# One cross attention of an eight-layer chain: four score products issued together, new instruction orders, and its last normalisation moved to GpSimd

## The chip, the core and the metric

One Trainium2 chip, one core. The metric is the device time of one execution in microseconds (us). The kernel does a whole chain of layers in one launch; the change touches a single phase of it, the cross attention called L1.

The engines have these names in the profile: PE is TensorE (matrix products), PEld its weight loads, DVE is VectorE, ACT is ScalarE, POOL is GpSimd. Each engine works through its own instruction list in order, and waits on semaphores that the others raise.

## The reference

x is 32 tiles of 128 tokens by 128 features, and ctx is of the same shape. The chain adds to x, layer by layer, a cross attention and a feed-forward network, four times. The L1 cross attention is:

```
q = layernorm(x) @ Wq.T ;  k = ctx @ Wk.T ;  v = ctx @ Wv.T      (16 heads of 8)
p = softmax(q k.T / sqrt(8))                                      (128 x 128 for each head)
x = x + concat(p v) @ Wo.T
```

The network that follows starts from layernorm(x), and this phase makes that normalised x too.

## The kernel before

All 32 tiles of x lie in on-chip memory (X). The phase `cross_attention_L1` works on one batch entry (a "tile", 128 x 128) at a time, and it is software-pipelined by hand. On every engine a function `step(n, ...)` lists the operations of one turn, each with its own offset: `maxima(n - 1, ...)` is the maxima of tile n-1, `norm(n + 1, ...)` the normalisation of tile n+1. `sequence_loop(engine, 32, lead, lag, step)` runs the turns. So the order of an engine is what `step` lists, and the offset says which tile it is for. Each helper waits on the semaphores of what it needs, and on those that say that the buffer it writes is free (most buffers have two copies, w = tile mod 2).

One tile goes through these operations (function, engine, line before):

- `statistics`, `aggregate` (DVE, L752, L757): mean and variance of a tile of x. `log_variance`, `over_deviation` (ACT, L696, L701): one over the deviation, through a logarithm and an exponential. `norm` (DVE, L763): the normalised tile; it waits for `over_deviation` of the same tile.
- `turn_x` (PE, L868): transpose. `evacuate_x` (DVE, L770): copy out of PSUM. `project` (PE, L875 to L877): q, k, v. `evacuate_fixed`, `evacuate_spread`, `evacuate_values` (DVE, L776, L782, L788): copies of the three. `turn_x` of the next tile waits for `evacuate_values` of this one, since both use one PSUM bank. `spread_heads`, `block_values`, `fetch_context` (POOL, L677, L670, L663): layouts for the products.
- `scores` (PE, L886): four products, one for each group g of four heads, into PSUM banks 0 to 3. Product g reads 32 rows of the array (rows 32g to 32g+31). The banks exist once, so product g of tile b needs the exponentials of group g of tile b-1 to be done.
- `maxima` (DVE, L794): row maxima of a group. `exponentials` (ACT, L719): four instructions for a group.
- `turn_probs` (PE, L897): four transposes for a group, into PSUM bank 4 or 5. `evacuate_probs`: copy out, for groups 0, 1, 2 on ACT (L728), for group 3 on DVE (L801).
- `weighted_values` (PE, L911): 64 small products; it needs all four copies. `one_over_rows`, `evacuate_heads` (DVE, L808, L814), `output` (PE, L919), `residual` (DVE, L819): x is updated.
- `statistics2`, `aggregate2` (DVE, L824, L829), `log_variance2`, `over_deviation2` (ACT, L706, L711), `end_norm` (DVE, L834): the normalised x for the next network.

Of the kernel before, what the change touches and what calls it, by code (L numbers as in the profile page):

```python
# [21 lines left out]
ALU = mybir.AluOpType  # L22
# [4 lines left out]
P = 128  # L27
# [548 lines left out]
def cross_attention_L1(nc, env, a):  # L576
# [55 lines left out]
    xn2_ready = sem("xn2_ready")  # L632
    probT3_ready = sem("probT3_ready")
# [15 lines left out]
    with nc.Block() as block:  # L649
# [5 lines left out]
        def _(pool):  # L655
# [23 lines left out]

            def step(n, u, live):  # L680
                v = 1 - u
                block_values(n, u, live)
                fetch_context(n + 1, v, live)
                spread_heads(n + 1, v, live)
            sequence_loop(pool, NB, 1, 0, step)
# [3 lines left out]
        def _(act):  # L689
# [18 lines left out]
            def over_deviation2(b, w, live):  # L708
                if live(b):
                    act.wait_ge(lnvar2_ready, b + 1)  # L710
                    nc.scalar.activation(rstd2[:, w:w + 1], lnvar2[:, w:w + 1], ACT.Exp, scale=-0.5).then_inc(rstd2_ready, 1)  # L711
# [19 lines left out]
            def step(n, u, live):  # L731
                v = 1 - u
                evacuate_probs(n + 1, v, 1, live)
                exponentials(n + 1, v, 3, live)
                log_variance(n + 4, u, live)
                over_deviation(n + 4, u, live)
                log_variance2(n - 1, v, live)
                evacuate_probs(n + 1, v, 2, live)
                over_deviation2(n - 1, v, live)
                exponentials(n + 2, u, 0, live)  # L740
                exponentials(n + 2, u, 1, live)
                exponentials(n + 2, u, 2, live)
                evacuate_probs(n + 2, u, 0, live)
            sequence_loop(act, NB, 4, 1, step)

        @block.vector
        def _(dve):
# [78 lines left out]
            def aggregate2(b, w, live):  # L826
                if live(b):
                    wait_alone(dve, env, stats2_ready, b + 1)
                    nc.vector.bn_aggr(moments2[:, w, :], stats2[:, w, :]).then_inc(moments2_ready, 1)  # L829

            def end_norm(b, w, live):
                if live(b):
                    dve.wait_ge(rstd2_ready, b + 1)
                    nc.vector.tensor_scalar(tile_of(NORMED, b), tile_of(X, b), moments2[:, w, 0:1], rstd2[:, w:w + 1],  # L834
                                            ALU.subtract, ALU.mult).then_inc(xn2_ready, 1)

            def step(n, u, live):
                v = 1 - u
                residual(n - 3, v, live)
                evacuate_values(n - 1, v, live)  # L840
                statistics2(n - 3, v, live)
                aggregate2(n - 3, v, live)
                statistics(n + 2, u, live)
# [4 lines left out]
                aggregate(n + 2, u, live)  # L848
                evacuate_x(n, u, live)
                maxima(n - 1, v, 3, live)  # L850
                one_over_rows(n - 2, u, live)
                evacuate_spread(n, u, live)
                evacuate_heads(n - 2, u, live)
                evacuate_fixed(n, u, live)
                end_norm(n - 4, u, live)
                norm(n + 1, v, live)
            sequence_loop(dve, NB, 2, 4, step)

        @block.tensor
        def _(pe):  # L860
# [18 lines left out]
            def scores(b, w, half, live):  # L879
                if live(b):  # L880
                    pe.wait_ge(spread_ready, b + 1)
                    pe.wait_ge(fixed_ready, b + 1)
                    for g in (2 * half, 2 * half + 1):
                        wait(pe, exp_ready, 4 * (b - 1) + g + 1)
# [36 lines left out]
            def step(n, u, live):  # L921
                v = 1 - u
                output(n - 3, v, live)
                turn_probs(n - 2, u, 2, live)
                scores(n - 1, v, 0, live)
                turn_x(n, u, live)
                turn_probs(n - 2, u, 3, live)
                scores(n - 1, v, 1, live)
                weighted_values(n - 2, u, live)
                project(n, u, live)  # L930
                turn_probs(n - 1, v, 0, live)
                turn_probs(n - 1, v, 1, live)
            sequence_loop(pe, NB, 0, 3, step)
# [2312 lines left out]
```

## Time and profile before

| | |
|---|---|
| median of three runs | 4469.63 us (4464.69 to 4471.03) |
| the profiled execution | 4465.72 us, span 4463.9 us |
| mean granted TensorE clock of the span | 0.96 |
| the L1 phase in the span | 307.6 to 560.3 us |
| PE, DVE, ACT, POOL busy in the span | 4153.5, 3762.2, 3604.0, 3147.1 us |

A timeline row is: start, busy time, engine, line, operation, output <- inputs, shapes, and how many like it were merged; in brackets the idle time before it and what ended it. Instructions overlap on one engine at their ends, so the time that one takes from the engine is read from start to start, while its length says when its result is there. The granted clock (PEclk) is 1.00 at 2.4 GHz and 0.50 at 1.2 GHz.

### The profile page before, as it was taken

The page shows a single profiled execution, that of the slowest core. Times are in us where ns is not written, and L with a number is a line of the kernel's source. Part 1 is how long each engine was busy: PE and PEld are TensorE (multiplying, and loading weights), DVE is VectorE, ACT ScalarE, POOL GpSimd, SP SyncE. Part 2 cuts the span into 40 slices and gives each one's busy share as a digit, 9 for nine tenths or more (in the row PEclk, how much of TensorE's full clock was granted, in tenths as well). Part 3 has the DMA queues.
Part 4 walks back from the last instruction along what each step waited for, and adds up shares of the span by engine and source line. Part 5 has one row for each costly group of instructions (what it writes and reads, how often), then busy time and mean ns, then how long its engine had stood idle before and what let it go on. Part 6 is the DMA issues. An engine that isn't in the chain of part 4 may idle for free. (4 is left out here: it accounts for less than half of the span.)

```text
span 4463.9 us, 151456 instructions
## 1 busy us (share of the span) xinstructions
PE 4153.5 (93%) x51003; PEld 2751.8 (62%) x51005; DVE 3762.2 (84%) x9029; ACT 3604.0 (81%) x12939; POOL 3147.1 (71%) x4201
## 2 busy tenths in 40 slices
PE   6949999999999999999999999999999999677885
PEld 3426656666666666666666666666666666455543
DVE  4779989889889889889888889889889885788497
ACT  6938878888888888888888888888888887688335
POOL 2422288888888888889888888888888885444162
PEclk9969999999999999999999999999999999788886
DMA  2000000000000000000000000000000000000000
GB/s 64 0 21 1 0 8 2 2 3 17 13 2 2 2 21 8 2 3 7 17 8 2 2 12 12 8 2 3 17 12 2 2 2 2 1 0 0 30 0 20
DMA packets 38631, 37.27 MB, mean 8 GB/s; under 512 B 11382, under 2 KB 30068, under 8 KB 37748
## 3 DMA queue, kind: packets, MB, share of 16 engines
q1 hardware_dynamic: 38004, 28.97, 2.3%
q8 instruction: 386, 6.32, 0.6%
q14 instruction: 241, 1.97, 0.1%
HBM read 26.86 MB, written 2.10 MB: 6 GB/s over the span
## 5 line engine op out<-in xcount | busy, mean ns | idle before, releaser
L2326 ACT ACTIVATE stack_prob<-ps,stack_shift_by 128x128 f32<-128x128 f32 x3072 | 1081.2, 378 | 3.3 <-DVE stack_shift_by L2448 2.7
L2254 POOL TENSOR_TENSOR stack_qk<-stack_qk,stack_rsin 128x512 f32<-128x512 f32 x768 | 970.8, 1275 | 41.1 <-DVE stack_rsin L2473 41.0
L2261 POOL TENSOR_TENSOR stack_qk<-stack_qk,stack_inv 128x512 f32<-128x512 f32 x768 | 794.8, 1046 | 217.8 <-ACT stack_inv L2345 217.8
L2646 PE MATMUL ps<-local_wqkv,stack_xsT 128*128 128x512 f32 x1536 | 797.1, 601 | 4.5 <-DVE stack_rsin L2473 2.4
L2268 POOL TENSOR_TENSOR stack_prob<-stack_prob,stack_rs 128x512 f32<-128x512 f32 x768 | 793.0, 1044 | 1.7 <-DVE stack_rs L2455 1.7
L2326 ACT ACTIVATION_READ_ACCUMULATOR stack_prob<-ps,stack_shift_by 128x1 f32 x3072 | 671.3, 219 | 1.3 <-issue 1.3
L2448 DVE TENSOR_REDUCE stack_shift_by<-ps 128x4 f32<-128x512 f32 x768 | 524.0, 682 | 77.2 <-PE ps L2725 71.9
L2473 DVE TENSOR_TENSOR stack_rsin<-ps,stack_sin_t 128x256 f32<-128x256 f32 x1536 | 571.9, 413 | 4.7 <-issue 4.7
L2462 DVE TENSOR_TENSOR stack_qk<-ps,stack_cos_t 128x512 f32<-128x512 f32 x768 | 525.2, 684 | 37.1 <-ACT stack_sq L2334 36.1
L2480 DVE TENSOR_REDUCE stack_ss<-stack_sq 128x8 f32<-128x512 f32 x768 | 513.3, 669 | 0.7 <-ACT stack_sq L2334 0.7
L2334 ACT ACTIVATE stack_sq<-ps 128x512 f32<-128x512 f32 x768 | 468.4, 610 | 52.8 <-PE ps L2646 45.3
L2306 ACT ACTIVATE stack_probT<-ps 128x512 f32<-128x512 f32 x768 | 428.7, 632 | 12.0 <-PE ps L2756 11.6
L2663 PE MATMUL ps<-local_wqkv,stack_xvT 128*128 128x512 f32 x768 | 432.9, 646 | 3.0 <-issue 3.0
L2776 PEld LDWEIGHTS ps<-stack_probT,stack_vals 128*64 128x64 f32 x6144 | 328.2, 136 | 162.2 <-issue 149.5
L2776 PE MATMUL ps<-stack_probT,stack_vals 128*64 128x128 f32 x6144 | 420.8, 279 | 5.8 <-issue 4.0
L2300 ACT ACTIVATE stack_qkT<-ps 128x512 f32<-128x512 f32 x384 | 231.4, 603 | 236.9 <-PE ps L2693 236.9
L2791 PE MATMUL ps<-local_wo,stack_oT 128*128 128x128 f32 x3072 | 389.0, 280 | 0.2 <-issue 0.2
L2791 PEld LDWEIGHTS ps<-local_wo,stack_oT 128*128 128x128 f32 x3072 | 361.2, 192 | 34.3 <-issue 24.5
L2646 PEld LDWEIGHTS ps<-local_wqkv,stack_xsT 128*128 128x128 f32 x1536 | 258.7, 191 | 173.4 <-issue 94.5
L2725 PE MATMUL ps<-stack_qkT 64*64 64x64 f32 (+1 forms) x12288 | 339.4, 230 | 0.0
L2725 PEld LDWEIGHTS ps<-stack_qkT 64*64 64x64 f32 x12288 | 307.2, 134 | 0.0
L2756 PEld LDWEIGHTS ps<-ident,stack_prob 64*128 64x128 f32 x6144 | 222.4, 139 | 93.9 <-issue 90.2
(342 smaller groups left out, 8606.0 us busy)
## 6 DMA issues: line engine op xcount, KB each, us to landing
local_wqkv<-L_ffn_Wqkv SPq DMA_DIRECT2D x30, 256.0 KB, 2.7
local_wo<-L_ffn_Wo SPq DMA_DIRECT2D x6, 512.0 KB, 4.6
out<-quantised_res SPq DMA_DIRECT2D x8, 256.0 KB, 2.3
local_w<-L_ffn_W SPq DMA_DIRECT2D x6, 341.0 KB
local_wqkv<-L_ffn_Wqkv SPq DMA_DIRECT2D x1, 1536.0 KB, 6.3
early_L_decay<-c_decay SPq DMA_DIRECT2D x1, 1024.0 KB, 10.0
local_w<-L_ffn_W SPq DMA_DIRECT2D x12, 64.0 KB
load_raw<-L_ffn_w SPq DMA_DIRECT2D x8, 64.0 KB, 1.9
```

What stands on the lines that cost most here:

```text
L2254: nc.gpsimd.tensor_tensor(qk[w][:, j, :, :], qk[w][:, j, :, :], rsin[j % 2][:, :, :], ALU.add).then_inc(rot_ready, 1)
L2261: nc.gpsimd.tensor_tensor(qk[w][:, j, :, :], qk[w][:, j, :, :], bcast(inv[:, w, 8 * j:8 * j + 8].unsqueeze(2), [P, 8, LH]), ALU.mult).then ...
L2268: nc.gpsimd.tensor_tensor(prob[w][:, g, :, :], prob[w][:, g, :, :], bcast(rs[:, w, HG * g:HG * g + HG].unsqueeze(2), [P, HG, P]), ALU.mult ...
L2326: last = nc.scalar.activation(prob[w][:, g, j, :], ps[:, 4 + g % 2, j * P:(j + 1) * P], ACT.Exp, bias=shift_by[:, w, h:h + 1], accum_out=s ...
L2448: nc.vector.tensor_reduce(shift_by[:, w, HG * g:HG * g + HG], bank, AX, ALU.max, negate=True).then_inc(shift_by_ready, 1)
L2462: nc.vector.tensor_tensor(qk[w][:, j, :, :], bank, bcast(cos_t[:, j // 2, :].unsqueeze(1), [P, 8, LH]), ALU.mult)
L2473: last = nc.vector.tensor_tensor(rsin[j % 2][:, :, o], bank[:, :, x], bcast(sin_t[:, j // 2, o].unsqueeze(1), [P, 8, 32]), ALU.mult)
L2480: nc.vector.tensor_reduce(ss[:, w, 8 * j:8 * j + 8, 0], sq[j % 2][:, :, :], AX, ALU.add).then_inc(ss_summed, 1)
L2646: nc.tensor.matmul(proj_bank(j), xsT[w][:, :], wqkv[:, 512 * j:512 * j + 512], start=True, stop=True).then_inc(proj_ready, 1)
L2725: last = nc.tensor.matmul(ps[part, 4 + p, j * P + keys.start:j * P + keys.stop], qkT[w][r, half, 0, j, part], qkT[w][r, half, 1, j, keys], ...
L2776: last = nc.tensor.matmul(PV[LH * p:LH * p + LH, j * P:(j + 1) * P], vals[w][:, LH * h:LH * h + LH], probT[w][:, 2 * half + p, j, :], star ...
L2791: last = nc.tensor.matmul(OUT[:, 0:P], oT[w][:, c, :], wo[:, c, :], start=c == 0, stop=c == 7)
```

## The change

1. `scores(b, w, half)` was called twice in a turn, for two groups each, with other PE work in between. Now `scores(b, w)` is called once, issues the four products one after the other, and first waits for all four exponentials of the tile before.
2. `end_norm` leaves DVE. POOL does it in two operations, a subtraction into a new buffer `centred` and a multiplication. Its semaphore is now also waited for by `aggregate2` and `over_deviation2`.
3. The lists of `step` on all engines are written anew, with new offsets.

```
@@ pool @@
+            def end_norm(b, w, live):
+                if live(b):
+                    pool.wait_ge(moments2_ready, b + 1)
+                    nc.gpsimd.tensor_tensor(centred[:, w, :], tile_of(X, b), bcast(moments2[:, w, 0:1], [P, P]),
+                                            ALU.subtract).then_inc(centred_ready, 1)
+                    wait_alone(pool, env, rstd2_ready, b + 1)
+                    wait_alone(pool, env, centred_ready, b + 1)
+                    nc.gpsimd.tensor_tensor(tile_of(NORMED, b), centred[:, w, :], bcast(rstd2[:, w:w + 1], [P, P]),
+                                            ALU.mult).then_inc(xn2_ready, 1)
             def step(n, u, live):
                 v = 1 - u
+                spread_heads(n + 1, v, live)
+                fetch_context(n + 2, u, live)
                 block_values(n, u, live)
-                fetch_context(n + 1, v, live)
-                spread_heads(n + 1, v, live)
-            sequence_loop(pool, NB, 1, 0, step)
+                end_norm(n - 3, v, live)
+            sequence_loop(pool, NB, 2, 3, step)
@@ scalar, over_deviation2 @@
+                    wait(act, xn2_ready, b - 1)
@@ scalar, step @@
-                evacuate_probs(n + 1, v, 1, live)
-                exponentials(n + 1, v, 3, live)
-                log_variance(n + 4, u, live)
-                over_deviation(n + 4, u, live)
-                log_variance2(n - 1, v, live)
-                evacuate_probs(n + 1, v, 2, live)
-                over_deviation2(n - 1, v, live)
                 exponentials(n + 2, u, 0, live)
                 exponentials(n + 2, u, 1, live)
                 exponentials(n + 2, u, 2, live)
                 evacuate_probs(n + 2, u, 0, live)
-            sequence_loop(act, NB, 4, 1, step)
+                exponentials(n + 2, u, 3, live)
+                evacuate_probs(n + 2, u, 1, live)
+                log_variance(n + 5, v, live)
+                evacuate_probs(n + 2, u, 2, live)
+                over_deviation(n + 5, v, live)
+                log_variance2(n, u, live)
+                over_deviation2(n, u, live)
+            sequence_loop(act, NB, 5, 0, step)
@@ vector, step (end_norm taken out above) @@
-                residual(n - 3, v, live)
-                evacuate_values(n - 1, v, live)
-                statistics2(n - 3, v, live)
-                aggregate2(n - 3, v, live)
-                statistics(n + 2, u, live)
                 maxima(n - 1, v, 0, live)
                 evacuate_probs(n - 2, u, 3, live)
                 maxima(n - 1, v, 1, live)
                 maxima(n - 1, v, 2, live)
-                aggregate(n + 2, u, live)
-                evacuate_x(n, u, live)
+                evacuate_spread(n, u, live)
                 maxima(n - 1, v, 3, live)
+                evacuate_fixed(n, u, live)
+                evacuate_values(n, u, live)
                 one_over_rows(n - 2, u, live)
-                evacuate_spread(n, u, live)
                 evacuate_heads(n - 2, u, live)
-                evacuate_fixed(n, u, live)
-                end_norm(n - 4, u, live)
-                norm(n + 1, v, live)
-            sequence_loop(dve, NB, 2, 4, step)
+                statistics(n + 3, v, live)
+                aggregate(n + 3, v, live)
+                norm(n + 2, u, live)
+                residual(n - 2, u, live)
+                evacuate_x(n + 1, v, live)
+                statistics2(n - 2, u, live)
+                aggregate2(n - 2, u, live)
+            sequence_loop(dve, NB, 3, 2, step)
@@ tensor @@
-            def scores(b, w, half, live):
+            def scores(b, w, live):
...
-                    for g in (2 * half, 2 * half + 1):
-                        wait(pe, exp_ready, 4 * (b - 1) + g + 1)
+                    wait_alone(pe, env, exp_ready, 4 * b)
+                    for g in range(G):
...
             def step(n, u, live):
                 v = 1 - u
-                output(n - 3, v, live)
-                turn_probs(n - 2, u, 2, live)
-                scores(n - 1, v, 0, live)
-                turn_x(n, u, live)
+                scores(n - 1, v, live)
                 turn_probs(n - 2, u, 3, live)
-                scores(n - 1, v, 1, live)
+                project(n, u, live)
                 weighted_values(n - 2, u, live)
-                project(n, u, live)
+                turn_x(n + 1, v, live)
                 turn_probs(n - 1, v, 0, live)
                 turn_probs(n - 1, v, 1, live)
-            sequence_loop(pe, NB, 0, 3, step)
+                output(n - 2, u, live)
+                turn_probs(n - 1, v, 2, live)
+            sequence_loop(pe, NB, 1, 2, step)
```

What this does to the order is seen best at the start of the phase, where the tiles can be counted. First DVE, from the last `norm` (L763, writes xn) ahead of the first maxima (L794, write shift_by) to the next `norm`, before the change. The first row is the norm of tile 1, the maxima are those of tile 0, and the last row is the norm of tile 2:

```order
L763 TENSOR_SCALAR L_cross_xn<-X,L_cross_moments,L_cross_rstd 128x128
L788 COPY L_cross_vals<-ps 128x128
L752 BN_STATS L_cross_stats<-X 128x6
L794 TENSOR_REDUCE L_cross_shift_by<-ps 128x4 x3
L757 BN_AGGR L_cross_moments<-L_cross_stats 128x2
L770 COPY L_cross_xnT<-ps 128x128
L794 TENSOR_REDUCE L_cross_shift_by<-ps 128x4
L782 TENSOR_SCALAR L_cross_spread_src<-ps 128x128
L776 COPY L_cross_fixed<-ps 128x128
L763 TENSOR_SCALAR L_cross_xn<-X,L_cross_moments,L_cross_rstd 128x128
```

The same piece of DVE after the change (norm is now L777, maxima L808). Three norms stand ahead of the first maxima, so the first row is the norm of tile 2, and the last row, which follows the maxima of tile 0, is the norm of tile 3:

```order
L777 TENSOR_SCALAR L_cross_xn<-X,L_cross_moments,L_cross_rstd 128x128
L784 COPY L_cross_xnT<-ps 128x128
L808 TENSOR_REDUCE L_cross_shift_by<-ps 128x4 x3
L796 TENSOR_SCALAR L_cross_spread_src<-ps 128x128
L808 TENSOR_REDUCE L_cross_shift_by<-ps 128x4
L790 COPY L_cross_fixed<-ps 128x128
L802 COPY L_cross_vals<-ps 128x128
L766 BN_STATS L_cross_stats<-X 128x6
L771 BN_AGGR L_cross_moments<-L_cross_stats 128x2
L777 TENSOR_SCALAR L_cross_xn<-X,L_cross_moments,L_cross_rstd 128x128
```

So in one turn DVE now has maxima(b) and norm(b+3), where it had maxima(b) and norm(b+2). The copy of the values moved from the end of the list to just behind the copy of q.

Second ACT, before the change, from the `log_variance` and `over_deviation` of tile 2 (L696, L701) over the exponentials of tile 0 (L719) and the copies of the turned probabilities (L728) to the pair of tile 3:

```order
L696 ACTIVATE L_cross_lnvar<-L_cross_moments,eps 128x1
L701 ACTIVATE L_cross_rstd<-L_cross_lnvar 128x1
L719 ACTIVATE L_cross_prob<-ps,L_cross_shift_by 128x128 x12
L728 ACTIVATE L_cross_probT<-ps 128x512 x2
L719 ACTIVATE L_cross_prob<-ps,L_cross_shift_by 128x128 x4
L696 ACTIVATE L_cross_lnvar<-L_cross_moments,eps 128x1
L701 ACTIVATE L_cross_rstd<-L_cross_lnvar 128x1
L728 ACTIVATE L_cross_probT<-ps 128x512
```

The same piece of ACT after the change (L709 and L714 are the pair, L733 the exponentials, L742 the copies):

```order
L709 ACTIVATE L_cross_lnvar<-L_cross_moments,eps 128x1
L714 ACTIVATE L_cross_rstd<-L_cross_lnvar 128x1
L733 ACTIVATE L_cross_prob<-ps,L_cross_shift_by 128x128 x12
L742 ACTIVATE L_cross_probT<-ps 128x512
L733 ACTIVATE L_cross_prob<-ps,L_cross_shift_by 128x128 x4
L742 ACTIVATE L_cross_probT<-ps 128x512
L709 ACTIVATE L_cross_lnvar<-L_cross_moments,eps 128x1
L742 ACTIVATE L_cross_probT<-ps 128x512
L714 ACTIVATE L_cross_rstd<-L_cross_lnvar 128x1
```

The pair of tile 3 still stands behind the exponentials of tile 0; its second half, on which `norm` of tile 3 waits, moved behind the third copy as well, and the second copy moved behind the last exponentials.

## Rows read from the trace of the kernel before

**Rows 1.** Windows: length, busy us (instructions) of PE, PEld, DVE, ACT, POOL; clock

```profile
400.00:440.00 40.00, 39.91 (x556) 27.75 (x556) 38.14 (x98) 35.98 (x128) 9.66 (x30) 1.00 0.00 0
```

**Rows 2.** Timeline of PE, one tile in the middle of the L1 phase

```profile
427.63 1.19 PE L886 MATMUL ps<-L_cross_spread,L_cross_fixed 32*128 32x512 f32 x4
428.75 0.33 PE L868 MATMUL ps<-ident,L_cross_xn 128*128 128x128 f32 x1
428.91 0.60 PE L897 MATMUL ps<-ident,L_cross_prob 128*128 128x128 f32 x4
...
430.50 1.08 PE L911 MATMUL ps<-L_cross_probT,L_cross_vbd 128*32 128x128 f32 x32
...
432.39 0.49 PE L875 MATMUL ps<-L_cross_xnT,L1WqT 128*128 128x128 f32 x2
...
434.03 0.39 PE L919 MATMUL ps<-L1WoT,L_cross_oT 128*128 128x128 f32 x2
434.45 0.66 PE L897 MATMUL ps<-ident,L_cross_prob 128*128 128x128 f32 x4
435.03 1.13 PE L886 MATMUL ps<-L_cross_spread,L_cross_fixed 32*128 32x512 f32 x4
```

**Rows 3.** Timeline of DVE at the same place

```profile
426.56 0.98 DVE L834 TENSOR_SCALAR Y<-X,L_cross_moments,L_cross_rstd  x1
427.46 0.33 DVE L763 TENSOR_SCALAR L_cross_xn<-X,L_cross_moments,L_cross_rstd 128x128 f32 x1
427.72 0.27 DVE L819 TENSOR_TENSOR X<-X,ps 128x128 f32 x1
427.92 0.28 DVE L788 COPY L_cross_vals<-ps 128x128 f32<-128x128 f32 x1
428.12 0.28 DVE L824 BATCH_NORM_STATS2 L_cross_stats<-X 128x6 f32 x1
...
428.64 0.29 DVE L752 BATCH_NORM_STATS2 L_cross_stats<-X 128x6 f32 x1
428.89 0.69 DVE L794 TENSOR_REDUCE L_cross_shift_by<-ps 128x4 f32<-128x512 f32 x1
...
430.16 1.28 DVE L794 TENSOR_REDUCE L_cross_shift_by<-ps 128x4 f32<-128x512 f32 x2
431.36 0.17 DVE L757 BATCH_NORM_AGGREGATE L_cross_moments<-L_cross_stats 128x2 f32<-128x6 f32 x1
```

**Rows 4.** Timeline of ACT at the same place

```profile
426.40 1.09 ACT L728 ACTIVATE L_cross_probT<-ps 128x512 f32<-128x512 f32 x2 [0.66 <-PE ps L897]
427.37 1.15 ACT L719 ACTIVATE L_cross_prob<-ps,L_cross_shift_by 128x128 f32<-128x128 f32 x4
428.37 0.33 ACT L696 ACTIVATE L_cross_lnvar<-L_cross_moments,eps 128x1 f32<-128x1 f32 x1
428.73 0.20 ACT L701 ACTIVATE L_cross_rstd<-L_cross_lnvar 128x1 f32<-128x1 f32 x1
428.84 0.28 ACT L706 ACTIVATE L_cross_lnvar<-L_cross_moments,eps 128x1 f32<-128x1 f32 x1
429.02 0.58 ACT L728 ACTIVATE L_cross_probT<-ps 128x512 f32<-128x512 f32 x1
```

**Rows 5.** Timeline of POOL and DVE: the last normalisation beside and without a POOL operation

```profile
426.42 1.04 POOL L677 TENSOR_TENSOR L_cross_spread<-L_cross_spread_src,head_rows 128x512 f32<-128x512 f32 x1 [4.41 <-DVE L_cross_spread_src L782]
...
551.54 0.34 DVE L834 TENSOR_SCALAR Y<-X,L_cross_moments,L_cross_rstd 128x128 f32<-128x128 f32 x1
```

**Rows 6.** Groups of instructions, other attentions: four-row-group products; a 128x128 POOL operation

```profile
L1643 PE MATMUL ps<-L_cross_spread,L_cross_fixed 32*128 32x512 f32 x256 | 39.3, 685 | 6.2 <-POOL L_cross_spread_aux L1347 4.5 <-issue 1.0
...
L366 POOL TENSOR_TENSOR L_cross_xb<-X,early_L_b_o 128x128 f32<-128x128 f32 x32 | 14.6, 455 | 0.0
```

**Rows 7.** Windows: the middle of the L2 attention

```profile
3900.00:4100.00 200.00, 155.77 (x2436) 114.97 (x2439) 172.92 (x410) 175.35 (x315) 94.45 (x251) 0.87 0.00 0
```

**Rows 8.** Timeline of PE at the start of the L1 phase, before the clock rose

```profile
314.31 2.08 PE L886 MATMUL ps<-L_cross_spread,L_cross_fixed 32*128 32x512 f32 x4 [1.50 <-POOL L_cross_spread L677]
```

More of the change, by code:

```diff
@@ L632, in cross_attention_L1 @@
     xn2_ready = sem("xn2_ready")
+    centred_ready = sem("centred_ready")
+    centred = sb("centred", [P, 2, P])
     probT3_ready = sem("probT3_ready")
@@ L827, in aggregate2 @@
                 if live(b):
-                    wait_alone(dve, env, stats2_ready, b + 1)
+                    waits_alone(dve, env, (stats2_ready, b + 1), (xn2_ready, b - 1))
                     nc.vector.bn_aggr(moments2[:, w, :], stats2[:, w, :]).then_inc(moments2_ready, 1)
[L831 to L835, printed above, removed]
             def step(n, u, live):
                 v = 1 - u
-                residual(n - 3, v, live)
-                evacuate_values(n - 1, v, live)
-                statistics2(n - 3, v, live)
-                aggregate2(n - 3, v, live)
-                statistics(n + 2, u, live)
                 maxima(n - 1, v, 0, live)
```

## The prediction

> **What bounds the kernel now.** I read the L1 phase in three steps: the windows of its middle, then the timelines of PE, DVE and ACT over one tile, then the idle times in them. The windows say that PE is busy 39.91 of 40 us, DVE 38.14 and ACT 35.98, at full clock [rows 1]. One tile takes from one first score product to the next, 427.63 to 435.03, so 7.40 us [rows 2]. PE works through nearly all of it. The only hole is at its end: `output` starts at 434.03 and the next transposes only at 434.45, though the tile before them left little to do. They wait for ACT's copy of group 0, and ACT had sat idle 0.66 us before that copy, waiting for PE's transposes [rows 4]. PE is the bound, with about 0.2 us of wait. DVE is close behind, and something there is dearer than it looks: the last normalisation at 426.56 keeps DVE for 0.90 us until the next starts at 427.46 [rows 3], while the same operation at the end of the phase lasts 0.34 us; in the first case POOL was in its `spread_heads` from 426.42 to 427.46 [rows 5]. So L834 stood still until POOL was through, and about 0.64 of its 0.90 us is that wait (0.90 less 0.26, what `norm` next to it takes [rows 3]).
>
> **What the change takes away.** (a) Score products. Two calls a tile take 1.12 us of PE each (427.63 to 428.75) [rows 2]. Four products on four row groups, issued together, are not in the L1 trace, but the L2 attention has them: 39.3 us for its 32 tiles, so 1.23 us for all four [rows 6], with its clock partly low. Bounds: no gain if they ran pair after pair (2.24), and 1.12 us if they take what a pair takes now. I take 1.1. (b) DVE loses the last normalisation, 0.90 us a tile, 0.26 if nothing had stood in its way. (c) POOL gains two operations of 128x128; 14.6 us for 32 such, 0.46 us each [rows 6]. POOL is busy 9.66 of 40 us [rows 1], so 1.8 a tile and then 2.7: no bound.
> The Trainium skill, "SBUF — State Buffer", section "SBUF: two separate sides", says that VectorE in a two-port mode and GpSimd take one port pair in turn, for a whole instruction. The trace agrees with 0.90 us beside POOL and 0.34 us without. Where DVE is the bound, that rule alone would make (b) worth 0.9 us a tile; it is part of rival A.
>
> **What the new orders put in.** This decides, and no busy time shows it: the offsets. Before, DVE's turn held the maxima of tile b and the `norm` of tile b+2; now it holds the maxima of b and the `norm` of b+3. `norm(b+3)` waits for `over_deviation(b+3)`. On ACT that stands, as before, behind the exponentials of tile b, and now also behind its third copy. Before, DVE asked for a value that ACT had made a tile earlier. Now it asks for one that ACT makes at the end of the same tile, after sixteen exponentials that themselves start from DVE's maxima. And behind the waiting `norm` on DVE stand `residual`, `evacuate_x`, the two of `statistics2`, and the maxima of tile b+1. So the turn becomes a ring, maxima(b) to maxima(b+1). Its length, start to start:
>
> - DVE, from the first maxima to the copy of the values: maxima and probability copy 1.27 (428.89 to 430.16), two maxima 1.20 (430.16 to 431.36), `evacuate_spread` 0.2, the fourth maxima 0.6, `evacuate_fixed` 0.2, and `evacuate_values` with its whole 0.28 [rows 3]: 3.75. The two 0.2 are the residual's start-to-start time, 427.72 to 427.92, since all are 128x128.
> - PE: `turn_x` must wait for that copy (one bank), then 0.16 (428.75 to 428.91), then the four transposes of group 0 of tile b, 0.60 until their result is there [rows 2]; with 0.05 for the hand-over, 0.81.
> - ACT: that group's copy 0.49 (two take 0.97, 426.40 to 427.37), the last exponentials 1.00 (427.37 to 428.37), a copy 0.49, the logarithm 0.18 (428.84 to 429.02), a copy 0.49, the exponential 0.20 [rows 4]; 2.85, and 0.04 of hand-over. Could ACT be later by its own work? From the maxima it is 0.69, three groups of exponentials 3.0: 3.7, before the 4.6 at which PE is done. So it waits for PE, some 0.8 us.
> - DVE again: `norm` 0.26 (427.46 to 427.72), `residual` 0.20, `evacuate_x` 0.2, `statistics2` with `aggregate2` 0.52 (428.12 to 428.64) [rows 3]; 1.18 and 0.04.
>
> Sum: 3.75 + 0.81 + 2.89 + 1.22 = 8.67. Each operation that I rounded up could be 0.03 less, so I take 8.6 us for a tile, against 7.4: **+1.2 us**. What the four products save on PE lies beside the ring. They start when the last exponentials of tile b are done and take 1.2 us with their result, while ACT needs 0.49 + 0.18 + 0.49 + 0.20 = 1.36 us more and DVE 1.2 after that. DVE reaches the next maxima 1.2 us after the products are ready. The 0.9 us off DVE falls into the new wait too: DVE is busy 38.14 of 40 us [rows 1], 7.1 us in 7.4, and 6.2 without the 0.9; of 8.6 us it then idles 2.4, some 2 of them at `norm`.
> `norm` waits like this for tiles 3 to 31, 29 times: 29 x 1.2 = **+35 us**.
>
> **Smaller terms.** The start: until its clock rises PE takes 2.08 us for a pair of score products [rows 8], and PE bounds there; one pair less for each of the first tiles, partly eaten by the ring: -3. The end: after the last statistics POOL does two dependent operations of 0.46 [rows 6] where DVE did one of 0.34 [rows 5]: +1. The clock: in the middle of L1 PE is busy 39.91 of 40 us at 1.00 [rows 1]; in the L2 attention it is busy 155.77 of 200 us and is granted 0.87 [rows 7], so it was at 1.2 GHz for a quarter of the time. With about 6.3 us of work (7.4 less 1.1) in 8.6 PE will be like that or a little busier. At half clock the ring gets another leg: maxima and copy 1.27, weighted values 1.89 (430.50 to 432.39) [rows 2] doubled to 3.8, then `turn_x` and transposes 1.4, in all 6.5 until ACT can copy, where the ring above has 4.6: +1.9 us for such a tile. Bounds: none, or a quarter of 29 tiles with all of it, 14 us. I take a tenth: +6.
> "TensorE: Matmul & The Clock Gate" of the Trainium skill, section "HAM oscillation — how this bites in real kernels", says that short stretches of products between waits are throttled anew each time. The windows of L2 agree. By that alone the clock term would be the upper bound.
>
> Sum: 35 - 3 + 1 + 6 = **+39 us**. Against the profiled execution's own 4465.72 us that is 4505; the median of the runs shown is 4469.63, 3.9 above it, so a median would be about 4508. Predicted: **4507 us**.
>
> **Rivals.**
> A, faster. The `norm` wait does not bind, because DVE asks later or ACT answers earlier than I read. Then PE has 7.40 - 1.1 - 0.2 = 6.1, DVE 7.4 - 0.9 = 6.5, ACT 7.4 - 0.66 = 6.7; and the banks make a ring of their own, since all four products wait for the last exponentials: 1.2 for the products, 0.69 for the first maxima, 4.0 of exponentials, one copy 0.49, and 0.4 of hand-overs, 6.8. So about 6.9 us a tile, 31 x -0.5 = -15 us: 4455. It decides if the wait at `norm` is under about 0.9 us a tile (2 less 1.2). For it: busy sums all fall. Against it: the order, in which no `over_deviation(b+3)` can come before the exponentials of tile b. Chance 0.08.
> B, no change: the wait binds, but ACT waits less for PE and the ring closes near 7.4. That needs 1.2 us out of 8.6, more than the whole 0.8 us wait in it. 0.04.
> C, the clock. L2's 0.87 or less in L1, with PE's share in the ring doubled for a quarter to half of the tiles: 14 to 28 us instead of 6, 4515 to 4530. 0.13.
> The forecast: 0.75.
>
> **Numbers.** A measurement of this kernel can tell about 0.2% (9 us) from no change. Faster 0.08, within 0.2% 0.04, slower 0.88. The ring's bounds: 8.45 to 8.7 us, so 31 to 38 us, and the clock 0 to 14: 4469.6 + 31 - 3 + 1 = 4498 to 4469.6 + 38 + 14 = 4522. Leaving two in ten outside, half of them on the side of A, I widen to 4488 and 4524.
>
> **What would show it.** In the timeline of the changed kernel's L1 phase: a tile takes 8.6 us; DVE idles about 2 us a tile before `norm` (now L777), released by ACT's `over_deviation` (L714), and that is the longest wait of the phase. ACT idles twice, once at the copy of group 0 (released by PE) and once before the first exponentials (released by the maxima). The four score products start within some 0.02 us of each other or in a row with a result after 1.2 us. PE idles 2 us a tile and its clock falls at times. POOL's two new operations last 0.46 us. Wrong would be: no idle time at L777, or a tile under 7.4 us; then A holds. Products that run pair after pair would be hidden behind the ring (0.3 us of it at most would show). If the tile takes 8.6 but the time is off, it is the clock term.

## The result and the profile after

The changed kernel takes 4519.78 us (median of five runs, 4514.52 to 4522.26) against 4469.63 (five runs, 4464.69 to 4471.03): ratio 1.011, 95% interval 1.0099 to 1.0121. It is slower, by 50 us, where 37 were predicted (4507; the prediction's own sum of terms was 39). The span of its profiled execution is 4518.0 us, 54.1 more than before's.

Where the 54.1 lie was read from the first and the last instruction of each phase. The L1 phase runs from 307.7 to 609.4, so 301.7 us where it took 252.7: +49.0. The layer stack behind it, whose code is the same, takes 5.3 more. Every other part differs by 0.9 at most, and all of them together by -0.2.

The windows of the changed kernel, as in [rows 1] and [rows 7]: a piece of the middle, the long stretch of equal tiles, and L2.

```profile
440.00:480.00 40.00, 30.14 (x410) 21.29 (x408) 26.65 (x74) 28.39 (x100) 10.52 (x32) 1.00 0.00 0
...
335.00:585.00 250.00, 188.60 (x2667) 136.57 (x2655) 173.01 (x463) 179.67 (x631) 72.55 (x222) 0.99 0.00 0
...
3900.00:4100.00 200.00, 157.93 (x2399) 116.48 (x2399) 171.07 (x408) 173.95 (x308) 91.01 (x247) 0.86 0.00 1
```

PE was busy 39.91 of 40 us [rows 1] and is now busy 30.14; DVE fell from 38.14 to 26.65. No engine is busy all the time any more. The tile grew by waiting, so the next view is the list of waits of 335 to 590 us (engine, line, who released it: us in total, times, longest):

```profile
DVE L_cross_xn L777 <- ACT L_cross_rstd L714: 64.0, 27, 2.8
ACT L_cross_prob L733 <- DVE L_cross_shift_by L808: 49.8, 28, 2.1
...
ACT L_cross_probT L742 <- PE ps L904: 17.5, 28, 1.6
...
PE ps L875 <- DVE L_cross_vals L802: 12.7, 27, 0.5
```

For each tile DVE waits at `norm` (L777) for ACT, 2.4 us; ACT waits at the copy (L742) for PE's transposes; PE waits at `turn_x` (L875) for DVE's copy of the values. These are the three hand-overs of a ring: a chain of waits that leads back to its own start, one tile later. ACT's wait for the maxima follows from the first, since the maxima stand behind `norm` on DVE. The timelines show it closed. DVE, one whole tile:

```profile
443.13 0.69 DVE L808 TENSOR_REDUCE L_cross_shift_by<-ps 128x4 f32<-128x512 f32 x1
...
446.52 0.28 DVE L802 COPY L_cross_vals<-ps 128x128 f32<-128x128 f32 x1
...
450.83 0.34 DVE L777 TENSOR_SCALAR L_cross_xn<-X,L_cross_moments,L_cross_rstd 128x128 f32 x1 [2.35 <-ACT L_cross_rstd L714]
...
452.48 0.69 DVE L808 TENSOR_REDUCE L_cross_shift_by<-ps 128x4 f32<-128x512 f32 x1 [0.43 <-issue]
```

PE and ACT between them:

```profile
446.95 0.30 PE L875 MATMUL ps<-ident,L_cross_xn 128*128 128x128 f32 x1 [0.48 <-DVE L_cross_vals L802]
447.16 1.09 PE L904 MATMUL ps<-ident,L_cross_prob 128*128 128x128 f32 x8
...
449.70 1.14 PE L893 MATMUL ps<-L_cross_spread,L_cross_fixed 32*128 32x512 f32 x8 [0.46 <-ACT L_cross_prob L733]
```

```profile
447.93 0.60 ACT L742 ACTIVATE L_cross_probT<-ps 128x512 f32<-128x512 f32 x1 [0.63 <-PE ps L904]
448.42 1.13 ACT L733 ACTIVATE L_cross_prob<-ps,L_cross_shift_by 128x128 f32<-128x128 f32 x4
...
450.56 0.24 ACT L714 ACTIVATE L_cross_rstd<-L_cross_lnvar 128x1 f32<-128x1 f32 x1
```

DVE from the first maxima to the end of the copy: 443.13 to 446.80, 3.67. PE until ACT can copy group 0: to 447.93, 1.13. ACT until `norm` starts: to 450.83, 2.90. DVE until it could take the next maxima: to 452.05, 1.22. That is 8.92. Then it idles 0.43 more, released by nothing but "issue", and this row comes at every second tile only. One turn of the hardware loop covers two tiles (`sequence_loop` runs `step` for u = 0 and 1), which is why the loop is suspected; e7 tries it. The tile shown is 9.35 us from first maxima to first maxima, its neighbours without the idle time are 9.00, mean 9.18, where tiles had a mean of 7.37. (Read from `norm` to `norm` the same tiles are 8.94 and 9.41; the expectation of e7 has them so.) 27 waits x 1.81 = 49 us, as much as the phase grew.

### The profile page after: what moved, and what is told of

Its sections match the earlier page's. It is cut to its first block and busy times, and to the rows that moved or that the text cites. A ratio compares the mean times of both kernels' runs of the same rounds, so it can differ in the third digit from the quotient of the medians.

```text
span 4518.0 us, 151512 instructions
## 1 busy us (share of the span) xinstructions
PE 4141.5 (92%) x51003; PEld 2752.0 (61%) x51005; DVE 3738.5 (83%) x8997; ACT 3600.3 (80%) x12939; POOL 3165.2 (70%) x4265
## 5 line engine op out<-in xcount | busy, mean ns | idle before, releaser
L2699 PE MATMUL ps<-ident,stack_qk 64*128 64x64 f32 x6144 | 274.6, 229 | 7.9 <-issue 6.3
```

## The experiments

All times are medians. Ratios are against the kernel before, run beside them: it took 4469.75 us beside e1 to e4, 4474.41 beside e5 to e8 and 4468.58 beside e9 to e11, so runs of different groups are compared by their ratios. "A tile" is the mean, first maxima to first maxima, of twenty tiles in the middle (tiles 5 to 24) of the profiled execution, in the changed kernel without the one that met 1.2 GHz; before 7.37. "L1" is the length of that phase in the profile, before 252.7.

| run | what it is | us | ratio (95%) | L1 | a tile |
|---|---|---|---|---|---|
| changed kernel | | 4519.78 | 1.011 (1.0099 to 1.0121) | 301.7 | 9.18 |
| e1_dev_early | over_deviation a tile earlier | 4479.25 | 1.0021 (1.0011 to 1.003) | 260.7 | 7.76 |
| e2_turnx_late | turn_x behind two groups of transposes | 4498.43 | 1.0062 (1.0047 to 1.0078) | 279.0 | 8.48 |
| e3_both | e1 and e2 | 4462.25 | 0.9984 (0.9975 to 0.9993) | 243.4 | 7.10 |
| e4_both_pairs | e3, products in two pairs | 4492.19 | 1.0045 (1.0029 to 1.006) | 269.5 | 7.96 |
| e5_both_dve_end | e3, last normalisation on DVE, tile n-3 | 4546.26 | 1.016 (1.0146 to 1.0174) | 323.1 | 10.14 |
| e6_before_pool_end | before, last normalisation on POOL | 4480.01 | 1.0009 (0.9999 to 1.0018) | 252.5 | 7.37 |
| e7_loop_rotated | changed kernel, DVE's loop begun at norm | 4521.01 | 1.0109 (1.0092 to 1.0125) | 297.1 | 9.09 |
| e8_both_rotated | e3, DVE's loop begun at norm | 4467.67 | 0.9984 (0.9974 to 0.9994) | 241.6 | 7.10 |
| e9_both_dve_end_late | e3, last normalisation on DVE, tile n-4 | 4458.48 | 0.9973 (0.9962 to 0.9985) | 243.3 | 7.11 |
| e10_after_dve_end | changed kernel, last normalisation on DVE, tile n-4 | 4515.36 | 1.0097 (1.0081 to 1.0112) | 298.1 | 9.14 |
| e11_before_four | before, four products together | 4497.8 | 1.0061 (1.0047 to 1.0074) | 280.8 | 8.22 |

**e1: cut the ring at norm.** On ACT, the pair that `norm` waits for is done for one tile later in the sequence, so a tile before DVE asks:

```
-                log_variance(n + 5, v, live)
+                log_variance(n + 6, u, live)
                 evacuate_probs(n + 2, u, 2, live)
-                over_deviation(n + 5, v, live)
+                over_deviation(n + 6, u, live)
...
-            sequence_loop(act, NB, 5, 0, step)
+            sequence_loop(act, NB, 6, 0, step)
```

> The changed kernel with one thing undone: on ScalarE the logarithm and the exponential for one over the deviation (log_variance, over_deviation) run one tile earlier (offset 6 in place of 5), so VectorE's norm finds its value made a tile ago. Theory of the ring (norm waits for the end of the same tile's ScalarE work): the wait before norm, 64 us over 27 tiles, goes; what is left of the ring (maxima, copy of the values, turn_x, transposes of group 0, their copy, last exponentials, four products) takes 3.7 + 1.1 + 0.5 + 1.0 + 1.3 = 7.6 to 7.7 us a tile against 8.94 now and 7.40 before: about 4478 us. Rival, the four products: they start only when all sixteen exponentials are done, and that alone costs the tile its time; then this edit changes little: over 4510 us. Rival, GpSimd's normalisation: also over 4510 us.

Its waits, 335 to 550 us:

```profile
DVE L_cross_shift_by L808 <- PE ps L893: 30.8, 28, 1.3
...
ACT L_cross_probT L742 <- PE ps L904: 16.1, 28, 0.6
PE ps L875 <- DVE L_cross_vals L802: 13.2, 28, 0.5
```

The row of `norm` is gone from the list, and DVE waits for the products instead. The phase loses 41.0 of its 49.0 us. This one offset is most of what the change costs; with all its other parts the kernel is 0.21% slower than before. Neither the products together nor POOL's normalisation, the two rivals, can be what holds it.

**e2: shorten the ring on PE.** `turn_x`, which holds up the transposes of groups 0 and 1 until DVE has copied the values, goes behind them:

```
-                turn_x(n + 1, v, live)
                 turn_probs(n - 1, v, 0, live)
                 turn_probs(n - 1, v, 1, live)
+                turn_x(n + 1, v, live)
                 output(n - 2, u, live)
```

> The changed kernel with one thing moved: on TensorE turn_x stands behind the transposes of groups 0 and 1, not ahead of them, so these no longer wait for VectorE's copy of the values. norm still waits for ScalarE. Ring theory: the leg over the copy of the values drops out, ScalarE works without its stop at the copy of group 0: 0.69 to the first exponentials, 3.0, 0.49, 1.0, 0.49 + 0.19 + 0.49 + 0.24 to the answer for norm, then 1.3 to the next maxima: 7.9 us a tile, 29 x 0.5 = 15 us over the kernel before: about 4484 us. If the wait of norm did not set the time at all but the copy of the values did, the tile would fall to about 7 us: 4455. If the four products set it: over 4510 us.

```profile
ACT L_cross_prob L733 <- DVE L_cross_shift_by L808: 46.6, 25, 2.1
DVE L_cross_xn L777 <- ACT L_cross_rstd L714: 42.0, 25, 1.7
```

ACT's wait for the transposes is gone and `norm` still waits, 1.7 us a tile. So the ring is there without PE's leg, as it should be. Its size was off: 8.48 us a tile and not 7.9, and L1 is 22.7 us shorter, where 36 were expected. The loop's turnaround, which was not in the estimate, is 0.44 at every second tile, 0.22 on the mean. In the tile that ends at 450.39, ACT also starts 0.82 after the first maxima and not 0.69, its twelve exponentials take 3.19 and not 3.0, and `norm` starts 0.47 after `over_deviation` and not 0.24.

**e3: both.** 

> Both edits together: the deviation a tile earlier on ScalarE, and turn_x behind the transposes of groups 0 and 1 on TensorE. Ring theory: neither leg is left; what bounds then is the ring of the PSUM banks (four products 1.2, first maxima 0.7, exponentials 4.0, one copy 0.5, hand-overs 0.4 = 6.8 to 6.9 us) with ScalarE's own 6.7 us just under it: 31 x 0.5 = 15 us under the kernel before: about 4454 us, the fastest. If one of the other rivals holds (products together, GpSimd's normalisation), it stays over 4470 us.

Neither wait is left. Tiles take 7.05 and 7.14 to 7.18 us, not the 6.8 to 6.9 of the expectation, and the kernel is 0.16% (7 us) under before and not 15; its interval ends below 1. Rival A's ring is 7.1 long here, from timeline starts: products to maxima 1.21, to the exponentials 0.82, these 3.23, the copy 0.49, the last exponentials 1.00, and 0.36 until the products start again. It is not alone. The products stand on PE behind `output`, which waits for DVE's copy of the heads:

```profile
449.95 0.49 PE L926 MATMUL ps<-L1WoT,L_cross_oT 128*128 128x128 f32 x2 [0.45 <-DVE L_cross_oT L828]
450.27 0.60 PE L904 MATMUL ps<-ident,L_cross_prob 128*128 128x128 f32 x4
450.92 1.14 PE L893 MATMUL ps<-L_cross_spread,L_cross_fixed 32*128 32x512 f32 x8
```

In the changed kernel the products start 0.15 after the last exponentials end (449.55 to 449.70). Here these end at 450.71, so by them alone the products could start at 450.86, 0.06 earlier than they do. The two paths are about as long, and no run tells them apart.

**e4: e3 with pairs.** The products are issued two and two again, the transposes of group 3 between them; both pairs still wait for all exponentials.

```
-                scores(n - 1, v, live)
+                scores(n - 1, v, 0, live)
                 turn_probs(n - 2, u, 3, live)
+                scores(n - 1, v, 1, live)
```

> The kernel with both edits, but the four score products are issued as two pairs again, with the transposes of group 3 between them, both pairs still only after all exponentials of the tile before. This prices the four together alone. If four on four row groups run in the time of two, the pairs cost TensorE 1.1 us more and the third and fourth maxima come later: about 7.9 us a tile, about 4484 us. If they run pair after pair anyway, no difference to the kernel with both edits.

PE, one pair, the transposes, the other pair:

```profile
443.31 1.13 PE L893 MATMUL ps<-L_cross_spread,L_cross_fixed 32*128 32x512 f32 x4
444.36 0.66 PE L904 MATMUL ps<-ident,L_cross_prob 128*128 128x128 f32 x4
444.95 1.13 PE L893 MATMUL ps<-L_cross_spread,L_cross_fixed 32*128 32x512 f32 x4
```

A pair takes 1.13 us, and all four together 1.14 (449.70 above, x8). In this order the four together are worth 0.86 us a tile, 26.1 us of the phase; the tile came out as expected.

**e5: last normalisation back on DVE, ahead of norm.** e3, with one operation on DVE for POOL's two:

```
                 aggregate(n + 3, v, live)
+                end_norm(n - 3, v, live)
                 norm(n + 2, u, live)
```

> The kernel with both orders mended (over_deviation a tile earlier on ACT, turn_x behind two groups of transposes), and the last normalisation back on VectorE (one operation, behind aggregate). Theory: GpSimd's two centring operations took 0.34 us of VectorE's tile away, and VectorE still waits some 0.5 us a tile for the products there, so that much of the added operation is hidden: +0 to +0.1 us a tile plus what a longer piece ahead of norm costs: 7.2 to 7.5 us a tile, 4465 to 4474. Rival (the port that GpSimd and VectorE share is what holds the norm): with GpSimd's operations gone the norm falls from 0.42-0.54 back to 0.32 us and the operation costs nothing net: 4455 to 4463.

Neither: 4546 us, the slowest of all. DVE's timeline (in the kernels with `end_norm` on DVE it is L837, norm L766, maxima L797, and L714 is `over_deviation2`):

```profile
431.80 0.18 DVE L760 BATCH_NORM_AGGREGATE L_cross_moments<-L_cross_stats 128x2 f32<-128x6 f32 x1
434.62 0.34 DVE L837 TENSOR_SCALAR Y<-X,L_cross_moments,L_cross_rstd  x1 [2.64 <-ACT L_cross_rstd L714]
434.88 0.34 DVE L766 TENSOR_SCALAR L_cross_xn<-X,L_cross_moments,L_cross_rstd 128x128 f32 x1
```

I had put the ring back myself. `over_deviation2(n-3)` is the last thing ACT does in the turn in which it does the exponentials of the tile whose maxima DVE has just made, and everything of DVE stood behind it. It is the changed kernel's fault, at another instruction. And the clock fell here:

```profile
335.00:590.00 255.00, 192.34 (x2449) 144.57 (x2449) 168.37 (x461) 165.69 (x586) 46.76 (x150) 0.91 0.00 0
```

The profile has 14 stretches at 1.2 GHz in these 255 us. From 347 us to 589 us the tiles without one take 9.05 to 9.36 us, as in the changed kernel, and those with one 10.3 to 11.0. So of the 10.14 about 9.2 is the ring and the rest is the clock.

**e9: the same, a tile later.** `end_norm(n - 4, u, live)` in the same place.

> The kernel with both orders mended, and the last normalisation on VectorE for tile n-4 (as before the change) instead of n-3. Theory (VectorE's wait at an operation whose value ScalarE makes at the end of the same tile is what costs, whichever operation it is): the value is a tile old, the ring of the run with n-3 is gone and with it all its 80 us: 7.1 to 7.3 us a tile, 4461 to 4470. Rival (the last normalisation costs on VectorE because VectorE itself is the bound in this order, 6.6 us busy of 7.1): 0.34 us a tile in full, 7.4 to 7.5, 4472 to 4476. Rival 2: something else made that run slow, and it stays above 4500.

```profile
442.33 0.35 DVE L837 TENSOR_SCALAR Y<-X,L_cross_moments,L_cross_rstd  x1
442.59 0.34 DVE L766 TENSOR_SCALAR L_cross_xn<-X,L_cross_moments,L_cross_rstd 128x128 f32 x1
...
444.03 0.69 DVE L797 TENSOR_REDUCE L_cross_shift_by<-ps 128x4 f32<-128x512 f32 x1 [0.22 <-PE ps L889]
```

One index: 0.0187 of the ratio, 84 us, of which 80 in the phase (323.1 to 243.3). The clock went back to 1.00 with it (335 to 540 us): by the tiles above some 57 us of the 80 are the ring (27 x 2.1, an estimate) and the rest is the clock, so the theory held, though it had all 80 in the ring. No wait stands before L837 now, and the tile is 7.11, as with POOL. The normalisation on DVE costs nothing, since DVE still idles before the maxima. This is the fastest kernel of the study. Against e3 it is not clearly faster: the intervals overlap and the L1 phases are equal (243.3 and 243.4).

**e10: the changed kernel with its last normalisation on DVE** (for tile n-4, ahead of `norm`). 

> The changed kernel with one part undone: the last normalisation back on VectorE, for tile n-4 and ahead of norm, the rest as changed. Theory: VectorE waits 2.4 us a tile at norm, the operation fits into that wait and costs nothing: 4515 to 4522, and the move to GpSimd was worth nothing there. Rival: 0.34 us a tile is added to the ring: 4529.

```profile
DVE L_cross_xn L766 <- ACT L_cross_rstd L703: 56.1, 27, 2.5
```

It fits into the wait at `norm`, which shrank from 64.0 to 56.1 us, and the tile is 9.14 against 9.18. The move to POOL was worth nothing there.

**e6: before with that part of the change alone.** 

> The kernel before with one part of the change alone: the last normalisation on GpSimd as two operations, everything else as before. Theory: VectorE's 0.34 to 0.9 us a tile were not on the path that sets the tile; the tile goes from 7.37 to about 7.3 us: 4465 to 4469, no change that can be told. Rival (VectorE is what bounds the tile before, at 38.14 of 40 us busy): 0.34 us x 30 = 10 us and more less: 4455 to 4460. Rival on the other side: GpSimd's operations stretch VectorE's beside them by 0.1 to 0.2 us: 4472 to 4476.

No change, as expected: the interval includes 1. The tile stays at 7.37, though DVE idles more in it (36.23 of 40 us busy where it was 38.14), so DVE's work was not the bound. But DVE did not get its 0.9 us either. `norm` (L777 here) over its 32 instructions, min/median/max in ns, and the place in the timeline:

```profile
L777 DVE TENSOR_SCALAR L_cross_xn<-X,L_cross_moments,L_cross_rstd x32: 346/974/1089, 313.5 to 540.4; 128x128 f32 x24, 128x128 f32<-128x128 f32 x8
```

```profile
422.43 1.04 POOL L679 TENSOR_TENSOR L_cross_spread<-L_cross_spread_src,head_rows 128x512 f32<-128x512 f32 x1 [4.53 <-DVE L_cross_spread_src L796]
422.57 0.98 DVE L777 TENSOR_SCALAR L_cross_xn<-X,L_cross_moments,L_cross_rstd 128x128 f32 x1
...
424.61 0.18 DVE L843 BATCH_NORM_AGGREGATE L_cross_moments<-L_cross_stats 128x2 f32<-128x6 f32 x1 [0.47 <-POOL Y L689]
```

Before, `end_norm` stood still beside POOL's `spread_heads` and `norm` took 0.33 [rows 3, 5]. With `end_norm` gone, `norm` comes to that place and stands still itself, 0.98. The two are the same operation on a tile of X, and touch no PSUM. Taking the first away hands its wait to the second. Not every DVE operation pays: `evacuate_fixed` starts at 426.37 before and is through in 0.28, and in the changed kernel the maxima and copies beside POOL's `spread_heads` (445.99 to 447.03) take 0.68 and 0.28, as elsewhere. And `aggregate2` waits 0.47 for POOL. What bounds the kernel before, PE by its busy time, was not tried by itself.

**e11: before with the four products together.** They stand where the first pair stood, and wait for all exponentials of the tile before; nothing else changes.

```
-                scores(n - 1, v, 0, live)
+                scores(n - 1, v, live)
                 turn_x(n, u, live)
                 turn_probs(n - 2, u, 3, live)
-                scores(n - 1, v, 1, live)
```

> The kernel before with one part of the change alone: the four score products of a tile together, where the first two stood, behind the last exponentials of the tile before; all other orders as before. Theory: the 1.1 us that TensorE saves is not all: every product now waits for the fourth group's exponentials, which before's ScalarE does behind two copies, so the new chain (products, first maxima, three groups of exponentials, copy, copy, the fourth group) sets the tile: 8.0 to 8.6 us, 4490 to 4506. Rival: TensorE was the bound, and its saving comes through: 6.6 to 7.0 us a tile, 4447 to 4459.

```profile
443.12 1.14 ACT L719 ACTIVATE L_cross_prob<-ps,L_cross_shift_by 128x128 f32<-128x128 f32 x4
...
444.41 1.14 PE L886 MATMUL ps<-L_cross_spread,L_cross_fixed 32*128 32x512 f32 x8 [0.95 <-ACT L_cross_prob L719]
...
445.64 0.69 DVE L794 TENSOR_REDUCE L_cross_shift_by<-ps 128x4 f32<-128x512 f32 x1 [0.96 <-PE ps L886]
...
446.45 3.33 ACT L719 ACTIVATE L_cross_prob<-ps,L_cross_shift_by 128x128 f32<-128x128 f32 x12 [1.01 <-DVE L_cross_shift_by L794]
```

The last exponentials release the products, these the maxima, these the next exponentials: 8.22 us a tile, inside the 8.0 to 8.6 expected. The same grouping that gains 26 us in e3's order loses 28 in before's. In before's order ACT does two copies ahead of the fourth group, in e3's one, and PE's transposes for them come early; which of the two does more was not tried.

**e7 and e8: where the loop turns around.** DVE's operations keep their order, but the body of the loop begins at `norm`:

```
             def step(n, u, live):
                 v = 1 - u
+                norm(n + 1, v, live)
+                residual(n - 3, v, live)
+                evacuate_x(n, u, live)
+                statistics2(n - 3, v, live)
+                aggregate2(n - 3, v, live)
                 maxima(n - 1, v, 0, live)
...
-                norm(n + 2, u, live)
-                residual(n - 2, u, live)
-                evacuate_x(n + 1, v, live)
-                statistics2(n - 2, u, live)
-                aggregate2(n - 2, u, live)
-            sequence_loop(dve, NB, 3, 2, step)
+            sequence_loop(dve, NB, 3, 3, step)
```

> The changed kernel with the same order of VectorE's operations, but the loop's body begins at norm and not at the first maxima, so that the loop's turnaround stands where VectorE waits for over_deviation anyway. Theory: the 0.47 us that every second tile is longer is the turnaround on the ring; all tiles take 8.94 us: 14 x 0.47 = 6.6 us less, 4513. Rival: the 0.47 us comes from what another engine's loop does (the turnarounds of TensorE or ScalarE), and the tiles still alternate 8.94 / 9.41: 4519.

> The kernel with both orders mended, and VectorE's loop begun at norm as well. Theory: there the ring is gone and the turnaround lies in VectorE's wait for the products (0.47 us a tile), so moving it to norm, where VectorE doesn't wait now, gains nothing: 4460 to 4465, as with the loop begun at the maxima. Rival: the turnaround is on whatever path sets the tile, and 0.1 us of each second tile comes back: 4457 to 4460.

```profile
449.51 0.34 DVE L777 TENSOR_SCALAR L_cross_xn<-X,L_cross_moments,L_cross_rstd 128x128 f32 x1 [2.58 <-ACT L_cross_rstd L714]
...
450.77 0.69 DVE L808 TENSOR_REDUCE L_cross_shift_by<-ps 128x4 f32<-128x512 f32 x1
```

The 0.43 before the maxima is gone, at both kinds of tile. But the tiles are 9.01 and 9.16 (`norm` to `norm`), not 8.94 all. What released that `norm` on ACT:

```profile
449.02 0.25 ACT L714 ACTIVATE L_cross_rstd<-L_cross_lnvar 128x1 f32<-128x1 f32 x1
```

`norm` starts 0.41 and 0.49 us after L714 starts, where it was 0.27 and 0.41 in the changed kernel (450.56 to 450.83). So some of the turnaround's work came back as a slower release. Half of the theory holds: the idle time before the maxima moves with DVE's loop, and no other engine's loop was touched. Its price can't be waited away in full: 0.09 us a tile came back of 0.22, some 3 us, which the times don't show (ratio 1.0109 against 1.011, and 6.6 us were expected). e8 came out as the theory had it: the ratio is e3's, and so are its tiles, 7.05 and 7.12 to 7.17.

## Why the prediction was right in sign and short in size

**The new ring, +35: right mechanism, 49 measured.** The chain of the prediction is the chain of the timeline, leg by leg: DVE 3.75 forecast and 3.67 measured, PE 0.81 and 1.13, ACT 2.89 and 2.90, DVE 1.22 and 1.22. e1 cuts it and 41 us come back; e5 and e9 make and cut it at another instruction, for some 57 (80 with the clock). 29 tiles were forecast to pay 1.2; the growth is that of 27 at 1.81. Two terms were mis-sized:

- The leg on PE, 0.81 where 1.13 was measured. It has one hand-over of 0.05, for which no row stands, where there are two. From DVE's copy to `turn_x` it is 0.15 (446.80 to 446.95), the next transposes start 0.21 later and not 0.16, and ACT starts 0.77 after the first of them, where the sum had 0.60 until the result and what was left of the 0.05. The hand-overs of 0.04 in the other legs have no row either.
- The loop's turnaround on DVE, which the sum lacked without a reason: 0.43 at every second tile, 0.22 on the mean. In the kernel before, whose loop on DVE begins at `residual`, no row shows it: `residual` follows `norm` after 0.26 [rows 3], and so in every tile of the middle.

The choice of 8.6 below the sum of 8.67, for operations that had been rounded up, took another 0.07 away. 0.32 + 0.22 + 0.07, less the 0.08 of DVE's first leg, is 0.53 of the 0.58 that 9.18 has over 8.6; most of the rest is that a tile without the idle time is 9.00 long, and not the 8.92 of the legs above.

**The products (a), saving hidden: right.** Four take 1.14 us where two took 1.13; in e9 their result is there after 1.22 (442.81 to 444.03). In the changed kernel they start at 449.70 and DVE comes for them at 452.48.

**DVE loses 0.90 (b), into the wait: right here, by e10.** But the 0.90 can't be had by moving `end_norm` alone. e6 shows the stall passing to `norm`, whose median is 974 ns there. "SBUF — State Buffer" of the Trainium skill, section "SBUF: two separate sides", has the port pair taken for a whole instruction, and e6 agrees: 0.98 beside POOL's 1.04, 0.35 for the shortest of the 32.

**POOL (c): right.** Its two operations take 0.40 each, 0.46 forecast, with 0.25 idle between them.

**The clock, +6: too much, about 1.** The granted clock was 0.99 over 335 to 585 us with PE busy 188.60 of 250, where L2 in the same trace is granted 0.86 with 157.93 of 200. In the middle only one tile met 1.2 GHz (434.6 to 438.0); it took 10.02 us from maxima to maxima instead of 9.00, so 1.0 more, where the prediction had 1.9 for such a tile and about three of them. Reading the clock of one phase off the busy share of another was the mistake. In e5 the same share of busy time, 192.34 of 255, came with 0.91. "TensorE: Matmul & The Clock Gate" of the Trainium skill, section "HAM oscillation — how this bites in real kernels", tells of a kernel in which each wait for a transfer is longer than the products before it. No phase here is like that: PE's longest idle time is 1.4 us in the middle of this kernel, 1.2 in e5 and 2.1 in L2, among longer stretches of products, and yet the clock fell in e5 and L2. So the section gives no price for this phase; what sets e5 apart from the changed kernel was not tried.

**Start and end, -3 and +1:** the first tile takes 7.37 where it took 9.04, so -1.7; from the last tile's first maxima to the end of the phase it is 15.3 where it was 13.5, so +1.7. The upper end that the prediction adds up, 4469.6 + 38 + 14, leaves these two terms out; with them it is 4520 and not 4522.

**Outside the phase:** 5 us that no term had, all in the layer stack. The prediction came from L1 alone and put this at nothing. Its code is the same in all kernels, and its length over before's was +5.3 (changed kernel), +1.7, +3.8, +5.3, +12.4, +14.3, +12.4, +2.4, +16.4, -1.1, +1.2 and -0.8 us (e1 to e11), with no relation to the edit that any run shows. The four that are over 12 are e4, e5, e6 and e8. The kernel before itself spread from 4467.23 to 4483.90 us beside e5 to e8, and from 4465.17 to 4475.03 beside e1 to e4. Some of it is the clock: within the stack the profile has 9.7 us at 1.2 GHz before, 25.8 in the changed kernel, 29.4 to 36.8 in those four, and 12.9 to 22.4 in the others. The changed kernel at the start of a layer:

```profile
1121.00:1124.00 3.00, 3.00 (x6) 1.44 (x5) 1.58 (x6) 1.81 (x11) 0.00 (x0) 0.50 0.02 5
```

Before has no such row at its place. Why it falls in one execution and not in another stays open, and so does how much of the differences of 5 to 6 us by the ratios (e3 to e9, changed kernel to e10) is this.

**Rival A** (faster, 4455) was a right picture of what lies behind the ring: 6.9 us a tile and 4455 us forecast, 7.1 in e3 and e9, 4462 and 4458 us. It needed an offset and a place of `turn_x` that this change doesn't have; the offset alone gives 7.76 (e1). B and C did not come: the ring closed above 7.4, and the clock stayed up.

## What to carry to other kernels

Check a reordered pipeline by its offsets before its busy sums: for every wait ask in which turn the other engine makes the value, and whether that turn itself started from something that is queued behind this wait. If yes it is a ring, and one index, not any engine's work, sets the time: here 41 us of a phase for one (e1) and 80 for another (e9), of which some 57 are the ring. Taking work off an engine is worth nothing while that engine waits in a ring anyway (e10), and the same grouping of products gains 26 us behind one order and costs 28 behind another (e4, e11).

## What the runs showed of the hardware

- The turnaround of DVE's loop shows as 0.43 us of idle time at its place in the changed kernel (L808, every second tile), and as none in the kernel before, where DVE has no long wait ahead of it; what hides it there was not tried. Moved to a place where the engine waits anyway, 0.13 of each 0.22 us a tile stayed, as a slower release.
- Four 32-row products of 512 columns on four row groups take 1.14 us, two take 1.13.
- A stall of DVE beside a POOL operation passes to the next like instruction: 0.98 us for `end_norm` before, 0.98 for `norm` when `end_norm` was gone. Maxima and copies out of PSUM beside the same POOL operation take 0.68 and 0.28, as elsewhere.
- PE idle for a quarter of the time kept 0.99 of its clock in one order (188.60 of 250 us busy) and 0.91 in another (192.34 of 255), with no idle time over 1.4 us in either.
